# The first stage of a transformer layer: outputs squared and gated bank by bank, chunk states by one scan, a new order

## The chip, the cores and the metric

The kernel runs on one core of one Trainium2 chip. The metric is the device time of one execution in microseconds (us), the median of several. The engines of a core run side by side, each through its own list of instructions, and wait for one another by semaphores: TensorE (PE; its weight loads PEld), VectorE (DVE), ScalarE (ACT), GpSimd (POOL) and SyncE (SP), which issues most transfers.

## The reference

A layer over 8 sequences of 1024 tokens of width 256, in fp32. The kernel's first stage computes the gated linear attention and the projections of the softmax attention behind it:

```python
q, k, v = heads(x @ Wq), heads(x @ Wk), heads(x @ Wv)      # x is layer-normalised; 4 heads, 32 wide (v: 64)
g = maximum(log_sigmoid(x @ Wgk1 @ Wgk2 + bgk2) / 16, -3)
# per head, over the 1024 tokens:
S = S * exp(g_t) + k_t (outer) v_t ;  o_t = q_t @ S
o = o * rsqrt(mean(o * o over a head) + EPS) * rms_w * silu(x @ Wg)
x = x + o @ Wout
# then: layer norm and RMS norm of x, and its products with wq, wk, wv
```

Later stages, which the change leaves alone, are the softmax attention, its output projection with the router, and the experts.

## The kernel before

The function is `gla_and_projections`. It works on 16 halves of a sequence (N = 16, 512 tokens each, T = 4 tiles of 128). Each engine's list is a loop `for n in bodies` with n from -2 to 16. In body n an engine works on several halves: the front part (normalised input, projections, gate, chunk states) of half n + 1, the back part (outputs, gating, output projection, `x1`, the q and k projections of the softmax attention) of half n, and the values and last roundings of half n - 1. The order in each list is written out by hand and is the order of execution; a waiting instruction holds back all that stand behind it on its engine.

A half is cut into NC = 16 chunks of C = 32 tokens. Within a chunk the outputs come from scores (`AT`), between chunks from states `S`. The names that matter:

- TensorE: `outputs` (lines 701 and 704, the products with the states `Sbd` and with `AT`, two tiles a bank), `projection` z, q, k, `values_and_gate` (line 619), `gated_transposes` of `o_s` and `attention_transposes` of `xr` (line 625), `output_projection` (724), `key_transposes` (661), `scores` (674), `increments` (686: each chunk's addition to the state, in 4 banks, 4 chunks a bank), `attention_projection` (619, `a_wT`), `values` (619, `a_wT,a_xrT`), `input_transposes` (625, `a_xn`).
- VectorE: `squares` (360), `outputs` (374 and 377: times the root, times the gate), `gates` and `running_sums` (392 is a scan), `layer_sum` (`x1` and its statistics, 406 to 413), `decayed` (`kt`, `qt`, 422 and 423), `attention_input` (`xr`, 430), `within_chunks` (440: scores into `AT` under a mask, by bank), `attention_input_low` (447), `states` (474), `rests` (482).
- ScalarE: the copies out of PSUM, the gate's Abs, Exp and Ln (219 to 223), the exponentials of the decays (251 to 255), `states` (278: four copies of 8 chunks each, one a head, into the block-diagonal `Sbd`, and again four), `rounded` (287).
- GpSimd: powers of -1/2 for the roots (548 to 567), `kh` and `qh`.

`states` on VectorE is a chain of 16 instructions, in which each reads the state before it and the increment in PSUM:

```python
V_.scalar_tensor_tensor(S[:, c + 1], S[:, c], decay[:, c:c + 1], p_f[:, c % 4, (c // 4) * DV:(c // 4 + 1) * DV],
                        ALU.mult, ALU.add).then_inc(s["S_step"], 1)
```

ScalarE starts on the first four copies of `Sbd` once 7 steps are done. TensorE's `outputs` of tiles 0 and 1 wait for these four, those of tiles 2 and 3 for the other four.

## Time and profile before

| | us |
|---|---|
| median of three runs (lowest, highest) | 3053.11 (3050.43, 3057.81) |
| span of the profiled execution | 3058.2 |
| first stage, in the span | 0 to about 735 |
| busy in the span: PE, DVE, ACT, POOL | 2879.5, 2283.9, 1938.1, 688.5 |

The profile is one execution, taken by the hardware profiler; beside its span there is nothing that it times. The span is read by stages. The softmax attention (735 to 2050) is the longest, the experts (2325 to 3058) the next. In the first stage the page's row of busy tenths shows PE at 9 and DVE and ACT at 5 to 7, and the granted TensorE clock mostly at 9 tenths. So the clock is not full there all the time.

### The profile page before, as it was taken

The page shows a single profiled execution, that of the slowest core. Times are in us where ns is not written, and L with a number is a line of the kernel's source. Part 1 is how long each engine was busy: PE and PEld are TensorE (multiplying, and loading weights), DVE is VectorE, ACT ScalarE, POOL GpSimd, SP SyncE. Part 2 cuts the span into 40 slices and gives each one's busy share as a digit, 9 for nine tenths or more (in the row PEclk, how much of TensorE's full clock was granted, in tenths as well). Part 3 has the DMA queues.
Part 4 walks back from the last instruction along what each step waited for, and adds up shares of the span by engine and source line. Part 5 has one row for each costly group of instructions (what it writes and reads, how often), then busy time and mean ns, then how long its engine had stood idle before and what let it go on. Part 6 is the DMA issues. An engine that isn't in the chain of part 4 may idle for free. (4 is left out here: it accounts for less than half of the span.)

```text
span 3058.2 us, 63018 instructions
## 1 busy us (share of the span) xinstructions
PE 2879.5 (94%) x22889; PEld 1806.1 (59%) x22890; DVE 2283.9 (75%) x4031; ACT 1938.1 (63%) x3559; POOL 688.5 (23%) x965
## 2 busy tenths in 40 slices
PE   5999999986999999999999999999888999999998
PEld 4777777774333333333333333337777888888886
DVE  5777777764999999999999999967785454545443
ACT  3666666661888888888888888875543333333332
POOL 2222222222000000000000000001103555555554
PEclk7899999986999999999999999998889999999999
DMA  1223323223222222222222222217642333333332
GB/s 45 87 98 107 111 101 105 100 84 117 68 74 65 83 72 72 67 67 65 73 72 69 66 64 72 73 39 212 213 146 51 50 50 50 49 51 49 50 50 42
DMA packets 170745, 243.05 MB, mean 79 GB/s; under 512 B 30920, under 2 KB 118240, under 8 KB 170512
## 3 DMA queue, kind: packets, MB, share of 16 engines
q1 hardware_dynamic: 121920, 170.57, 18.4%
q0 software_dynamic: 31152, 52.33, 8.9%
q10 hardware_dynamic: 17440, 16.98, 1.7%
q8 instruction: 155, 2.54, 0.4%
q14 instruction: 78, 0.64, 0.1%
HBM read 126.53 MB, written 111.21 MB: 78 GB/s over the span
## 5 line engine op out<-in xcount | busy, mean ns | idle before, releaser
L1030 DVE TENSOR_REDUCE b_mxq<-b_p_m 128x1 f32<-128x1024 f32 x1024 | 1220.6, 1222 | 76.2 <-PE b_p_m L1057 67.2
L964 ACT ACTIVATE b_probs<-b_p_e 128x512 f32<-128x512 f32 x2048 | 1105.4, 597 | 140.7 <-PE b_p_e L1110 40.1
L1057 PE MATMUL b_p_m<-b_kst,b_qst 64*128 64x512 f32 x1536 | 568.2, 449 | 0.8 <-DVE b_mxq L1030 0.8
L1110 PE MATMUL b_p_e<-b_qst,b_kst 64*128 64x512 f32 x1536 | 559.6, 444 | 0.2 <-ACT b_probs L964 0.2
L1082 PE MATMUL b_p_o<-b_probs,b_vst 128*32 128x256 f32 x6160 | 481.9, 390 | 0.5 <-ACT b_probs L964 0.4
L1110 PEld LDWEIGHTS b_p_e<-b_qst,b_kst 64*128 64x128 f32 x1536 | 236.4, 184 | 312.3 <-ACT b_probs L964 266.0
L1849 ACT ACTIVATE d_act<-d_p_up 128x512 f32<-128x512 f32 x136 | 81.2, 597 | 490.7 <-PE d_p_up L1922 490.7
L1082 PEld LDWEIGHTS b_p_o<-b_probs,b_vst 128*32 128x32 f32 x6160 | 126.3, 108 | 243.4 <-issue 133.4
L1818 POOL DMA_INDIRECT out_dram<-d_y,d_to x136 | 217.7, 1601 | 216.8 <-DVE d_y L1883 204.1
L1937 PE MATMUL d_p_y<-w2T,d_hT 128*128 x1096 | 259.1, 379 | 0.8 <-ACT d_hT L1843 0.8
L1865 DVE TENSOR_SCALAR d_xh<-d_p_x,d_ln 128x128 fp32r<-128x128 f32 x272 | 82.9, 346 | 233.5 <-PE d_p_x L1916 233.5
L1922 PE MATMUL d_p_up<-up_hi,d_xh 128*128 x544 | 248.7, 457 | 3.5 <-DVE d_xl L1869 1.5
L1057 PEld LDWEIGHTS b_p_m<-b_kst,b_qst 64*128 64x128 f32 x1536 | 234.3, 185 | 15.7 <-DVE b_mxq L1030 12.4
L1937 PEld LDWEIGHTS d_p_y<-w2T,d_hT 128*128 128x128 f32 x1096 | 207.9, 190 | 34.7 <-issue 1.0
L1922 PE MATMUL d_p_up<-up_hi,d_xl 128*128 x544 | 216.2, 397 | 0.0
L1922 PE MATMUL d_p_up<-up_lo,d_xh 128*128 x544 | 215.3, 396 | 0.0
L1057 PE MATMUL b_p_m<-kst,qst 64*128 64x512 f32 x512 | 194.3, 463 | 10.1 <-DVEq L1021 7.6
L1110 PE MATMUL b_p_e<-qst,kst 64*128 64x512 f32 x512 | 187.0, 444 | 0.2
L1008 POOL DMA_DIRECT2D o_d<-b_oT x63 | 35.7, 567 | 658.1 <-ACT b_oT L954 658.1
L1883 DVE TENSOR_SCALAR d_y<-d_p_y,d_share 128x256 f32<-128x256 f32 x137 | 66.3, 484 | 127.7 <-PE d_p_y L1937 118.4
L1082 PE MATMUL b_p_o<-b_probs,vst 128*32 128x256 f32 x2048 | 160.3, 390 | 0.0
L1806 POOL DMA_INDIRECT d_xs<-xg_d,d_tok x133 | 134.0, 1007 | 109.2 <-POOL d_tok L1803 103.3
(319 smaller groups left out, 4628.5 us busy)
## 6 DMA issues: line engine op xcount, KB each, us to landing
b_qst<-qk_d SPq DMA_DIRECT2D x288, 64.0 KB
b_kst<-qk_d SPq DMA_DIRECT2D x288, 64.0 KB
qk_d<-a_hi SPq DMA_DIRECT2D x32, 512.0 KB, 2.8
qk_d<-a_lo SPq DMA_DIRECT2D x32, 512.0 KB, 3.8
v_d<-a_v_s SPq DMA_DIRECT2D x16, 1024.0 KB, 4.5
o_d<-b_oT POOLq DMA_DIRECT2D x63, 256.0 KB, 2.7
b_vst<-v_d SPq DMA_DIRECT2D x48, 256.0 KB
raw<-in_L_ffn_w_dram SPq DMA_DIRECT2D x24, 512.0 KB, 4.9
```

Of the source, the lines that this page charges most:

```text
L964: nc.scalar.activation(probs[(2 * step + e % 4 // 2) % BUFS][:, (e % 2) * 512:(e % 2 + 1) * 512], p_e[(slot(e) if more1 else e) % EB][:], ...
L1030: V_.reduce_max(mxq[half][:, h, qt:qt + 1], p_m[j % 2][:], AX.X).then_inc(s["m_red"], 1)
L1057: mm(p_m[j % 2][:, kh * 512:(kh + 1) * 512], qst[r][rows(h), qt * P:(qt + 1) * P], kst[r][rows(h), kh * 512:(kh + 1) * 512], start=True, s ...
L1082: last = mm(p_o[32 * (2 * h + a):32 * (2 * h + a) + 32, at:at + 256], vst[step // KT % RING][:, step % KT, h, :], probs[(2 * step + h) % B ...
L1110: mm(p_e[u % EB][:], kst[r][rows(h), kt * P:(kt + 1) * P], qst[r][rows(h), a * 512:(a + 1) * 512], start=True, stop=True).then_inc(s["e_ps ...
L1806: g.indirect_dma_start(xs[r][:], None, xg_d, bass.IndirectOffsetOnAxis(ap=tok[r][:, 0:1], axis=0)).then_inc(s[f"x_in{r}"], 16)
L1818: g.indirect_dma_start(out_d, bass.IndirectOffsetOnAxis(ap=to[r][:, 0:1], axis=0), y[r][:], None, compute_op=ALU.add).then_inc(s[f"y_out{r ...
L1849: nc.scalar.activation(act_s[r][:], p_up[r][:, 0], ACT.Silu).then_inc(s["act_done"], 1)
L1865: last = V_.tensor_scalar(xh[r][:, k], p_x[:, k], ln2[:, k:k + 1], None, ALU.mult)
L1883: V_.tensor_scalar(y[1 - r][:], p_y[:, 0:D], share[(q + 3) % 4][:, 0:1], None, ALU.mult).then_inc(s["y_done"], 1)
L1922: last = mm(p_up[r][:, u], x[r][:, k], w[:, bass.ds(e, 1), u, k, :].rearrange("p o n -> p (o n)"), start=(j == 0), stop=(j == 5))
L1937: last = mm(p_y[:, 0:D], hT[r][:, k], w2T[:, bass.ds(e, 1), k, :].rearrange("p o n -> p (o n)"), start=(k == 0), stop=(k == 3))
```

## The change

1. `outputs` raises a semaphore for each bank of two tiles. ScalarE squares bank by bank (`output_squares(n, 0)`, `(n, 1)`), VectorE sums bank by bank, and multiplies the outputs by the gate straight out of PSUM (`gated_outputs`); ScalarE's copy to `o_s` is gone. Roots are taken in halves, and the product with them comes last.
2. The states come from one scan of VectorE. `S`, `steps` and `added` have the shape [P, DV, NC + 1], the chunk innermost. ScalarE writes the decays to `steps` (repeated over the 64 values) and the increments to `added` (four copies, one a bank). The first column of each row of `steps` is 0 and that of `added` the carried state, so one scan over 64 x 17 = 1088 elements gives all states. ScalarE's eight copies to `Sbd` read `S` with the chunk outside and the value inside, which is a step of 17 floats, and all wait for the scan.
3. ScalarE loads the table set that holds both exp and ln ahead of the gate; Silu needs the other. That makes 2 table loads a body in place of 4.
4. TensorE's `values(n - 1, 1)` moves from between the q and k projections to behind the key transposes, and z goes ahead of `values(n - 1, 0)`. `attention_transposes` goes tile by tile, each tile after its own `xr`. GpSimd's `input_roots` finishes the root that `xr` needs before it begins the other.
5. The orders on ScalarE, VectorE and SyncE follow. `rounded(n, 2)` moves to the next body, behind the first squares; `layer_norm` moves to the next body.
6. The mask is built in `o2`, whose space is free at the start.

The core of the diff:

```diff
-    S = sb("S", [P, NC + 1, DV])
+    S, steps, added = (sb(n, [P, DV, NC + 1]) for n in ("S", "steps", "added"))
...
             store_projection(n - 1, 1, "st_k")
-            store_values(n - 1)
             if n == N - 1:
                 load_first_pair()
             store_sum(n)
+            store_values(n - 1)
...
-        def output_squares(h):
-            if not 0 <= h < N:
-                return
-            act.wait_ge(s["o_ps"], h + 1)
-            A.activation(o2[:].rearrange("p t d -> p (t d)"), p_g[:, 0:2].rearrange("p a c -> p (a c)"), ACT.Square, scale=DV ** -0.5).then_inc(s["o2_done"], 1)
-
-        def outputs(h):
-            if not 0 <= h < N:
-                return
-            A.copy(o_s[:].rearrange("p t d -> p (t d)"), p_g[:, 0:2].rearrange("p a c -> p (a c)")).then_inc(s["o_s_done"], 1)
-
-        def gate(f):
+        def output_squares(h, part):
+            if not 0 <= h < N:
+                return
+            act.wait_ge(s["o_ps"], 2 * h + part + 1)
+            A.activation(o2[:, 2 * part:2 * part + 2].rearrange("p t d -> p (t d)"), p_g[:, part], ACT.Square, scale=DV ** -0.5).then_inc(s["o2_done"], 1)
+
+        def gate_table(f):
+            if not 0 <= f < N:
+                return
+            A.preload_act_table_set("natural_log_exp_and_others")
...
+            act.wait_ge(s["cum_done"], f + 1)
+            A.activation(e_cum[:], cum[:], ACT.Exp)
+            A.activation(decay[:], cum[:].rearrange("p (c j) -> p c j", j=C)[:, :, C - 1], ACT.Exp).then_inc(s["exps"], 1)
             act.wait_ge(s["tail_done"], f + 1)
             A.activation(e_tail[:], tail[:], ACT.Exp).then_inc(s["exps_tail"], 1)
-            A.activation(e_out[:], rel[:], ACT.Exp, scale=-1.0)
-            A.activation(e_in[:], rel[:], ACT.Exp).then_inc(s["exps_rel"], 1)
-            A.activation(e_cum[:], cum[:], ACT.Exp)
-            A.activation(decay[:], cum[:].rearrange("p (c j) -> p c j", j=C)[:, :, C - 1], ACT.Exp).then_inc(s["exps"], 1)
+            act.wait_ge(s["rel_done"], f + 1)
+            A.activation(e_in[:], rel[:], ACT.Exp)
+            A.activation(e_out[:], rel[:], ACT.Exp, scale=-1.0).then_inc(s["exps_rel"], 1)
+
+        def decay_steps(f):
+            if not 0 <= f < N:
+                return
+            act.wait_ge(s["exps"], f + 1)
+            A.copy(steps[:, :, 1:], decay[:].rearrange("p (o c) -> p o c", o=1).to_broadcast([P, DV, NC])).then_inc(s["steps_done"], 1)
+
+        def increments(f):
+            if not 0 <= f < N:
+                return
+            if f > 0:
+                act.wait_ge(s["S_done"], f)
+            for c in range(4):
+                act.wait_ge(s["inc_ps"], 4 * f + c + 1)
+                last = A.copy(added[:, :, 1:].rearrange("p v (t b) -> p b t v", b=4)[:, c], p_f[:, c, 0:T * DV].rearrange("p (t v) -> p t v", t=T))
+            last.then_inc(s["added_done"], 1)
...
-            act.wait_ge(s["S_step"], f * NC + 8 * part + 7)
+            act.wait_ge(s["S_done"], f + 1)
             for h in range(H):
-                last = A.copy(Sbd[h * DK:(h + 1) * DK, 8 * part:8 * part + 8, h * DV:(h + 1) * DV], S[h * DK:(h + 1) * DK, 8 * part:8 * part + 8, :])
+                last = A.copy(Sbd[h * DK:(h + 1) * DK, 8 * part:8 * part + 8, h * DV:(h + 1) * DV], S[h * DK:(h + 1) * DK, :, 8 * part:8 * part + 8].rearrange("p v c -> p c v"))
...
         for n in bodies:
+            input(n + 1)
+            output_squares(n, 0)
+            rounded(n - 1, 2)
             rounded(n - 1, 3)
-            input(n + 1)
-            output_squares(n)
+            gate_table(n + 1)
+            output_squares(n, 1)
+            gate_absolute(n + 1)
             values(n - 1, 0)
-            outputs(n)
-            gate(n + 1)
-            values(n - 1, 1)
-            q_k(n + 1)
+            gate_exponential(n + 1)
+            query(n + 1)
+            gate_logarithm(n + 1)
+            key(n + 1)
             gated(n)
             decays(n + 1)
             values_and_gate(n + 1, range(T))
             keys(n + 1)
+            values(n - 1, 1)
+            decay_steps(n + 1)
             attention_input(n)
+            increments(n + 1)
             rounded(n, 0)
             rounded(n, 1)
             states(n + 1, 0)
-            rounded(n, 2)
             states(n + 1, 1)
...
-        def squares(h):
-            if not 0 <= h < N:
-                return
-            dve.wait_ge(s["o2_done"], h + 1)
-            V_.reduce_sum(ss[:], o2[:].rearrange("p t (h v) -> p (t h) v", h=H), AX.X).then_inc(s["ss_done"], 1)
+        def squares(h, part):
+            if not 0 <= h < N:
+                return
+            dve.wait_ge(s["o2_done"], 2 * h + part + 1)
+            V_.reduce_sum(ss[:, 8 * part:8 * part + 8], o2[:, 2 * part:2 * part + 2].rearrange("p t (h v) -> p (t h) v", h=H), AX.X).then_inc(s["ss_done"], 1)
+
+        def gated_outputs(h, part):
+            if not 0 <= h < N:
+                return
+            dve.wait_ge(s["o_ps"], 2 * h + part + 1)
+            dve.wait_ge(s["vg_taken"], h * T + T)
+            V_.tensor_tensor(o_s[:, 2 * part:2 * part + 2].rearrange("p t d -> p (t d)"), p_g[:, part],
+                             G[h % 2][:, 2 * part:2 * part + 2].rearrange("p t d -> p (t d)"), ALU.mult).then_inc(s["oG_done"], 1)
...
-        def outputs(h):
-            if not 0 <= h < N:
-                return
-            dve.wait_ge(s["rs_done"], h + 1)
-            dve.wait_ge(s["o_s_done"], h + 1)
-            ov = o_s[:].rearrange("p t (h v) -> p (t h) v", h=H)
-            V_.tensor_tensor(ov, ov, rs[:].rearrange("p (a o) -> p a o", o=1).to_broadcast([P, T * H, DV]), ALU.mult).then_inc(s["on_done"], 1)
-            dve.wait_ge(s["on_done"], h + 1)
-            dve.wait_ge(s["vg_taken"], h * T + T)
-            V_.tensor_tensor(o_s[:], o_s[:], G[h % 2][:], ALU.mult).then_inc(s["og_done"], 1)
+        def outputs(h, part):
+            if not 0 <= h < N:
+                return
+            dve.wait_ge(s["rs_done"], 2 * h + part + 1)
+            dve.wait_ge(s["oG_done"], 2 * h + part + 1)
+            ov = o_s[:, 2 * part:2 * part + 2].rearrange("p t (h v) -> p (t h) v", h=H)
+            V_.tensor_tensor(ov, ov, rs[:, 8 * part:8 * part + 8].rearrange("p (a o) -> p a o", o=1).to_broadcast([P, 2 * H, DV]), ALU.mult).then_inc(s["og_done"], 1)
...
-                last = V_.tensor_scalar(xr[:, t], x1[:, t], mvb[:, t, 0:1], roots[:, 1, t:t + 1], ALU.subtract, ALU.mult)
-            last.then_inc(s["xr_done"], 1)
+                V_.tensor_scalar(xr[:, t], x1[:, t], mvb[:, t, 0:1], roots[:, 1, t:t + 1], ALU.subtract, ALU.mult).then_inc(s["xr_done"], 1)
...
+        def carried(f):
+            if not 0 <= f < N:
+                return
+            if f > 0:
+                dve.wait_ge(s["S_done"], f)
+            if f % 2:
+                V_.tensor_copy(added[:, :, 0], S[:, :, NC]).then_inc(s["S_carry"], 1)
+            else:
+                V_.memset(added[:, :, 0], 0.0).then_inc(s["S_carry"], 1)
+
         def states(f):
-            if not 0 <= f < N:
-                return
-            dve.wait_ge(s["inc_ps"], f + 1)
-            dve.wait_ge(s["exps"], f + 1)
+
+            if not 0 <= f < N:
+                return
+            dve.wait_ge(s["S_carry"], f + 1)
+            dve.wait_ge(s["steps_done"], f + 1)
+            dve.wait_ge(s["added_done"], f + 1)
             if f > 0:
                 dve.wait_ge(s["Sbd_done"], 2 * f)
-            if f % 2:
-                dve.wait_ge(s["S_step"], f * NC)
-                V_.tensor_copy(S[:, 0], S[:, NC]).then_inc(s["S_carry"], 1)
-            else:
-                V_.memset(S[:, 0], 0.0).then_inc(s["S_carry"], 1)
-            for c in range(NC):
-                if c > 0:
-                    dve.wait_ge(s["S_step"], f * NC + c)
-                else:
-                    dve.wait_ge(s["S_carry"], f + 1)
-                V_.scalar_tensor_tensor(S[:, c + 1], S[:, c], decay[:, c:c + 1], p_f[:, c % 4, (c // 4) * DV:(c // 4 + 1) * DV],
-                                        ALU.mult, ALU.add).then_inc(s["S_step"], 1)
+            flat = [tile[:].rearrange("p v c -> p (v c)") for tile in (S, steps, added)]
+            V_.tensor_tensor_scan(flat[0], flat[1], flat[2], 0.0, ALU.mult, ALU.add).then_inc(s["S_done"], 1)
...
+            input_low(n + 1)
+            squares(n, 0)
+            gated_outputs(n, 0)
             rests(n - 1, (2, 3))
             if n + 2 > 0:
                 statistics(n + 2)
-            input_low(n + 1)
-            squares(n)
+            squares(n, 1)
+            gated_outputs(n, 1)
+            layer_norm(n - 1)
             gate_minimum(n + 1)
-            outputs(n)
+            outputs(n, 0)
+            outputs(n, 1)
             gates(n + 1)
             running_sums(n + 1)
             if n + 2 > 0:
...
             layer_sum(n)
             decayed(n + 1)
             attention_input(n)
+            carried(n + 1)
             within_chunks(n + 1)
             attention_input_low(n)
-            layer_norm(n)
             states(n + 1)
             rests(n, (0, 1))
...
-            g.tensor_scalar(roots[:, 1], mvb[:, :, 1], 1.0 + EPS, EPS * EPS, ALU.mult, ALU.add)
+            g.tensor_scalar(roots[:, 1], mvb[:, :, 1], 1.0 + EPS, EPS * EPS, ALU.mult, ALU.add).then_inc(s["roots_eps"], 1)
+            pool.wait_ge(s["roots_eps"], 2 * h + 1)
+            g.tensor_tensor(roots[:, 1], roots[:, 1], mhalf[:, 0:T], ALU.pow).then_inc(s["roots_done"], 1)
             g.tensor_scalar(roots[:, 0], mvb[:, :, 1], EPS, None, ALU.add).then_inc(s["roots_eps"], 1)
-            pool.wait_ge(s["roots_eps"], h + 1)
-            g.tensor_tensor(roots[:, 1], roots[:, 1], mhalf[:, 0:T], ALU.pow).then_inc(s["roots_done"], 1)
+            pool.wait_ge(s["roots_eps"], 2 * h + 2)
             g.tensor_tensor(roots[:, 0], roots[:, 0], mhalf[:, 0:T], ALU.pow).then_inc(s["root0_done"], 1)
...
-                pe.wait_ge(s["S_step"], f * NC)
+                pe.wait_ge(s["added_done"], f)
...
-            last.then_inc(s["inc_ps"], 1)
+                last.then_inc(s["inc_ps"], 1)
...
-            pe.wait_ge(s["og_done"], h + 1)
+            pe.wait_ge(s["og_done"], 2 * h + 2)
             if h > 0:
-                pe.wait_ge(s["v_done"], 2 * h)
+                pe.wait_ge(s["v_done"], 2 * h - 1)
+                pe.wait_ge(s["lo_done"], 4 * h)
...
-            pe.wait_ge(s["xr_done"], h + 1)
-            transposes(p_g[:, 2:4], xr, s["xrT_ps"], each=True)
+            if h > 0:
+                pe.wait_ge(s["v_done"], 2 * h)
+            for t in range(T):
+                pe.wait_ge(s["xr_done"], h * T + (t + 1))
+                for k in range(2):
+                    last = tr(p_g[:, 2 + k, t * P:(t + 1) * P], xr[:, t, k * P:(k + 1) * P], ident[:])
+            last.then_inc(s["xrT_ps"], 1)
...
         for n in bodies:
             outputs(n, (0, 1))
             outputs(n, (2, 3))
+            projection(n + 1, "z", 2, "z_ps")
             values(n - 1, 0)
-            projection(n + 1, "z", 2, "z_ps")
             projection(n + 1, "q", 0, "q_ps")
-            values(n - 1, 1)
             projection(n + 1, "k", 1, "k_ps")
             values_and_gate(n + 1, 0)
             gated_transposes(n)
...
             values_and_gate(n + 1, 2)
             values_and_gate(n + 1, 3)
             key_transposes(n + 1)
+            values(n - 1, 1)
             scores(n + 1)
             attention_transposes(n)
             increments(n + 1)
```

**TensorE, from the vg projections to the increments.** `a_wT,a_xrT` in a product 256 wide is `values`. Before:

```order
L724 MATMUL a_p_g<-a_Wout_s,a_ogT 128x256 x8
L619 MATMUL a_p_f<-a_W_f,a_xT 128x512 x4
L619 MATMUL a_p_f<-a_W_f,a_xTl 128x512 x2
L619 MATMUL a_p_f<-a_W_f,a_xT 128x512 x4
L619 MATMUL a_p_f<-a_W_f,a_xTl 128x512 x2
L661 MATMUL a_p_f<-a_ident,a_kh 128x128 x4
L674 MATMUL a_p_f<-a_qt,a_kt 128x128 x16
L625 MATMUL a_p_g<-a_ident,a_xr 128x128 x8
L686 MATMUL a_p_f<-a_V,a_khat 32x64 x64
```

The same place of the changed kernel, whose lines have other numbers:

```order
L670 MATMUL a_p_f<-a_W_f,a_xTl 128x512 x2
L711 MATMUL a_p_f<-a_ident,a_kh 128x128 x4
L670 MATMUL a_p_g<-a_wT,a_xrT 128x256 x4
L670 MATMUL a_p_g<-a_wT,a_xrTl 128x256 x2
L670 MATMUL a_p_g<-a_wT,a_xrT 128x256 x4
L670 MATMUL a_p_g<-a_wT,a_xrTl 128x256 x2
L724 MATMUL a_p_f<-a_qt,a_kt 128x128 x16
L785 MATMUL a_p_g<-a_ident,a_xr 128x128 x8
L736 MATMUL a_p_f<-a_V,a_khat 32x64 x64
```

Twelve matmuls of the earlier half's values now stand between the key transposes and the scores.

**ScalarE, from the copy of `khat` to the next body's first copies.** `a_hi` is `rounded`, `a_xT` the next half's input, `a_o` the squares. Before:

```order
L261 COPY a_khat<-a_p_f 128x512
L268 ACTIVATE a_xrT<-a_p_g,a_ln1w_s 128x512 x2
L287 CAST a_hi<-a_p_g 128x512 x2
L278 COPY a_Sbd<-a_S 32x8x64 x4
L287 CAST a_hi<-a_p_g 128x512
L278 COPY a_Sbd<-a_S 32x8x64 x4
L287 CAST a_hi<-a_p_g 128x512
L202 CAST a_xT<-a_p_f 128x1024
L208 ACTIVATE a_o<-a_p_g 128x1024
```

Now:

```order
L291 COPY a_khat<-a_p_f 128x512
L326 COPY a_v_s<-a_p_g 128x8x2x16 x2
L275 COPY a_steps<-a_decay 128x64x16
L298 ACTIVATE a_xrT<-a_p_g,a_ln1w_s 128x512 x2
L284 COPY a_added<-a_p_f 128x4x64 x4
L317 CAST a_hi<-a_p_g 128x512 x2
L308 COPY a_Sbd<-a_S 32x8x64 x8
L202 CAST a_xT<-a_p_f 128x1024
L208 ACTIVATE a_o<-a_p_g 128x512
L317 CAST a_hi<-a_p_g 128x512 x2
```

The copies to `steps` and `added` are new, the eight `Sbd` copies stand together, and two roundings have gone behind the next half's first copies.

**VectorE, from `kt` and `qt` to the rests.** Before:

```order
L422 TENSOR_TENSOR a_kt<-a_k_s,a_e_out 128x512
L423 TENSOR_TENSOR a_qt<-a_q_s,a_e_in 128x512
L430 TENSOR_SCALAR a_xr<-a_x,a_mvb,a_roots 128x256 x4
L440 COPY_PREDICATED a_AT<-a_maski,a_p_f 128x512 x4
L447 SCALAR_TENSOR_TENSOR a_xrTl<-a_p_g,a_ln1w_s,a_xrT 128x512 x2
L454 COPY norm<-a_roots 128x4
L455 SCALAR_TENSOR_TENSOR norm<-a_mvb,a_roots 128x4
L468 MEMSET a_S 128x64
L474 SCALAR_TENSOR_TENSOR a_S<-a_S,a_decay,a_p_f 128x64 x16
L482 TENSOR_TENSOR a_lo<-a_p_g,a_hi 128x512 x4
```

Now:

```order
L464 TENSOR_TENSOR a_kt<-a_k_s,a_e_out 128x512
L465 TENSOR_TENSOR a_qt<-a_q_s,a_e_in 128x512
L472 TENSOR_SCALAR a_xr<-a_x,a_mvb,a_roots 128x256 x4
L504 COPY a_added<-a_S 128x64
L481 COPY_PREDICATED a_AT<-a_maski,a_p_f 128x512 x4
L488 SCALAR_TENSOR_TENSOR a_xrTl<-a_p_g,a_ln1w_s,a_xrT 128x512 x2
L518 SCALAR_TENSOR_TENSOR a_S<-a_steps,a_added 128x1088
L525 TENSOR_TENSOR a_lo<-a_p_g,a_hi 128x512 x2
```

One scan (shown here as SCALAR_TENSOR_TENSOR, as the other scan is) stands where the 16 steps stood.

## Rows read from the trace of the kernel before

**Rows 1.** Timeline of TensorE, one body: start us, length us, instructions, [wait before]

```profile
393.76 0.64 PE L701 MATMUL a_p_g<-a_Sbd,a_qh 128*32 128x256 f32 x8
...
404.36 0.64 PE L619 MATMUL a_p_g<-a_wT,a_xrT 128*128 128x256 f32 x4
...
405.80 1.10 PE L619 MATMUL a_p_f<-a_xT,a_W_f 128*128 128x512 f32 x4
...
414.40 1.28 PE L619 MATMUL a_p_f<-a_W_f,a_xT 128*128 128x512 f32 x4
...
417.40 0.60 PE L661 MATMUL a_p_f<-a_ident,a_kh 128*128 128x128 f32 x4
419.15 1.17 PE L674 MATMUL a_p_f<-a_qt,a_kt 32*128 32x128 f32 x32 [1.15 <-DVE a_qt L423]
422.68 1.47 PE L625 MATMUL a_p_g<-a_ident,a_xr 128*128 128x128 f32 x8 [2.35 <-DVE a_xr L430]
...
426.71 2.07 PE L619 MATMUL a_p_g<-a_xrT,a_wT 128*128 128x512 f32 x4
...
432.49 1.07 PE L619 MATMUL a_p_g<-a_xrT,a_wT 128*128 128x512 f32 x4
...
433.85 1.04 PE L625 MATMUL a_p_f<-a_ident,a_xn 128*128 128x128 f32 x8
434.81 0.64 PE L701 MATMUL a_p_g<-a_Sbd,a_qh 128*32 128x256 f32 x8
```

**Rows 2.** Stretches: length, busy of PE, PEld, DVE, ACT, POOL; granted clock; DMA

```profile
420.30:422.70 2.40, 0.05 (x4) 0.03 (x1) 2.40 (x5) 0.00 (x0) 2.17 (x2) 1.00 0.15 50
...
426.70:429.40 2.70, 2.70 (x10) 2.15 (x7) 2.27 (x9) 0.00 (x0) 0.00 (x0) 0.50 0.02 6
```

**Rows 3.** Timeline of VectorE in the same body

```profile
418.37 0.68 DVE L423 TENSOR_TENSOR a_qt<-a_q_s,a_e_in 128x512 f32<-128x512 f32 x1
420.29 2.33 DVE L430 TENSOR_SCALAR a_xr<-a_x,a_mvb,a_roots 128x256 f32<-128x256 f32 x4 [1.24 <-POOL a_roots L566]
422.54 2.57 DVE L440 COPY_PREDICATED a_AT<-a_maski,a_p_f 128x512 f32<-128x512 int32 x4
425.02 1.38 DVE L447 SCALAR_TENSOR_TENSOR a_xrTl<-a_p_g,a_ln1w_s,a_xrT 128x512 fp32r<-128x512 f32 x2
```

**Rows 4.** Timeline of GpSimd in the same body

```profile
418.56 0.58 POOL L564 TENSOR_SCALAR a_roots<-a_mvb 128x4 f32<-128x4 f32 x1
419.22 1.04 POOL L566 TENSOR_TENSOR a_roots<-a_roots,a_mhalf 128x4 f32<-128x4 f32 x1
```

**Rows 5.** Timeline of ScalarE in the same body

```profile
431.85 2.49 ACT L278 COPY a_Sbd<-a_S 32x512 f32<-32x512 f32 x4
```

**Rows 6.** Groups by line and shape: count | busy us, mean ns of one | wait

```profile
L550 POOL TENSOR_TENSOR a_rs<-a_rs,a_mhalf 128x16 f32<-128x16 f32 x16 | 46.9, 2930 | 1.3
L392 DVE TENSOR_TENSOR_SCAN a_cum<-a_keep,a_zm 128x512 f32<-128x512 f32 x16 | 19.6, 1225 | 0.5
L360 DVE TENSOR_REDUCE a_ss<-a_o 128x16 f32<-128x1024 f32 x16 | 19.6, 1222 | 25.7 <-ACT a_o L208 25.7
L254 ACT ACTIVATE a_e_cum<-a_cum 128x512 f32<-128x512 f32 x16 | 9.8, 615 | 0.0
L255 ACT ACTIVATE a_decay<-a_cum 128x16 f32<-128x16 f32 x16 | 3.4, 214 | 0.0
...
L1396 DVE TENSOR_REDUCE slots<-c_where 128x8 f32<-128x64 f32 x16 | 4.3, 268 | 0.5
...
L1288 ACT ACTIVATE c_ed<-c_diff 128x4 f32<-128x4 f32 x16 | 3.1, 193 | 7.5 <-DVE c_diff L1368 7.5
```

**Rows 7.** Stretches, as in rows 2: `outputs` in body 0 and in body 1

```profile
58.90:70.40 11.50, 11.50 (x65) 7.88 (x65) 1.22 (x1) 1.29 (x2) 0.00 (x0) 0.50 0.00 0
106.30:112.60 6.30, 6.30 (x66) 4.45 (x65) 3.75 (x11) 4.00 (x7) 0.00 (x0) 1.00 0.48 179
```

**Rows 8.** Timeline of TensorE in body 15, where the gated transposes begin

```profile
700.39 0.90 PE L625 MATMUL a_p_g<-a_ident,a_o_s 128*128 128x128 f32 x3 [5.34 <-DVE a_o_s L377]
```

51 lines of the change are left out of this document (30 added, 21 removed).

## Prediction

> **What bounds the kernel now.** I read the page first, then TensorE's timeline of one body, then the clock by stretch, then the engines it waits for. The change touches only the first stage, whose body runs 15 times from n = 0 to n = 14 with all its parts. Its start, the first matmul of `outputs`, stands at 393.76 and again at 434.81, so a body takes 41.05 us [rows 1]. The profile's span is 3058.2 us, 5.1 us (0.17%) over the median of the runs; I work out a saving on the span and take it from the median.
>
> In a body TensorE is nearly always busy. It waits twice: 1.15 us ahead of the scores (for `qt`) and 2.35 us ahead of the transposes of `xr` [rows 1]. Inside the second wait the granted clock is still 1.00; from 426.70 to 429.40, in the first attention projection, it is 0.50 [rows 2]. The fourth projection takes 1.36 us (432.49 to 433.85), which is full clock; all four take 7.14 (426.71 to 433.85) instead of 5.44 [rows 1]. So a body loses 3.5 us to waits and at least 1.7 us to the clock. Nothing else holds TensorE; a gain has to come out of these 5.2 us.
>
> **What the change does there.** All times from here are counted from E, the end of the output projection (414.40 in the trace).
>
> Before: `qt` is ready at E + 4.65 and the scores run from there; `roots` at E + 5.86; the four `xr` at E + 5.89 to 8.22; transposes from E + 8.28; increments to E + 12.31; then projections, input transposes, and the next `outputs` at E + 20.41 [rows 1, 3, 4].
>
> *The moved product.* `values(n-1, 1)` took 1.44 us (404.36 to 405.80) ahead of E [rows 1]. It now fills the wait ahead of the scores: vg and key transposes end at about E + 3.6, the product at E + 5.05, just after `qt` (E + 4.65). The stretch ahead of E shortens by 1.44, and the first wait is gone. The scores end at E + 6.2.
>
> *Roots and `xr`.* GpSimd now does one preparatory step less ahead of the first pow: 0.66 us (418.56 to 419.22) [rows 4]. `xr` starts at E + 5.25 and each quarter takes 0.58, since GpSimd is busy beside it as before; the last ends at E + 7.58. Transposes go tile by tile, so only two are left then: they end at E + 7.85, with waits of 0.7 in all.
>
> *Chunks and increments.* The four predicated copies (2.57 us, [rows 3]) follow at E + 7.8, after a small carry copy, and end at E + 10.35. A bank of increments waits for each. Increments never ran at full clock in a body; between 0.3 and 0.65 a bank, I take 0.65, since 2.6 us for four is what the half-clock row shows and the copies set the pace anyway. They end at E + 11.05 against 12.31.
>
> *If TensorE alone decided,* four projections at full clock and the input transposes (5.44 + 0.96) put the next `outputs` at E + 17.5 (before 20.41), and with the 1.44 the body would be 36.7 us: 4.4 less.
>
> *The state chain, which decides next.* The 16 steps were interleaved with the Sbd copies. Now the increments are copied to `added` (last bank E + 11.5), the scan waits for that and for `xrTl` (E + 10.35 + 1.38), and then all eight Sbd copies wait for the whole scan. The scan over 1088 elements costs 1225 x 1088/512, less fixed cost, about 2.45 [rows 6]: done at E + 14.2. ScalarE first rounds the second projection (E + 14.5). Then come the eight copies.
>
> *What one copy costs now.* A copy takes 0.62 us reading `S` in order (2.49 for four, [rows 5]). Now it reads with a step of 17 floats. Two rows show such reads. ScalarE's `decay` reads 16 elements 32 floats apart in 214 ns; 4 elements in order take 193 and 512 take 615, which puts 16 in order at 203: 0.7 ns more per element. VectorE's reduction over 64 elements 8 floats apart takes 268 ns; from 0.68 us at 512 and 1222 at 1024, 64 in order would take about 214: 0.84 ns more per element [rows 3, 6]. For 512 elements that is 0.36 to 0.43 us on top, so a copy costs 0.98 to 1.05; the other bound is no surcharge, 0.62. Both rows point the same way, so I take 1.04.
>
> The Trainium skill (SBUF — State Buffer, the note on cachelines in the section on the DMA port swizzle) says that each access that crosses to a new 16-byte line pays a penalty. The two rows agree for reads. By that page the writes to `added` would pay as well, some 0.2 us on the chain a body, which no row shows.
>
> With 1.04, four copies end at E + 18.7 and eight at E + 22.9. `outputs` of tiles 0 and 1 can start at 18.7, those of tiles 2 and 3 wait until 22.9, and end 3.1 later at E + 26.0 (before: 20.41 + 6.30 = 26.7). From there to the next E it is 14.33 - 1.44 = 12.9. The body: 38.9 us, 2.15 less. So TensorE's two old waits shrink and a new one of about 2.2 us stands ahead of and inside `outputs`.
>
> *The rest lies beside other work.* Squaring and gating by bank saves one ScalarE pass over the outputs and adds fixed costs on VectorE; with the pow in halves (2930 ns for 16 columns, 1.04 for 4: about 1.7 for 8) the gated outputs are ready about when the gated transposes come, within 0.3 us either way. Two of four table loads go from ScalarE, beside TensorE's projections: nothing. The `steps` copy (1024 elements, about 1.0) fits into ScalarE's wait for the `xrT` transposes. The queue of stores moves one store behind another, with its ring free for most of a body: nothing. VectorE loses 5 us of steps and gains 2.45.
>
> *Ends of the stage.* In body 15 nothing hides the chain from outputs to gated transposes, 8.3 us before (to 700.39 [rows 8]); square and reduction of half the data, half the pow and one multiplication make it about 4.3. Earlier roots and `xr` by tile save about 1 more. The start gains nothing, since eight slow copies take the place of the interleaved ones. Together 5.
>
> **Sum.** 15 x 2.15 + 5 = 37: 3058.2 - 37 = 3021.2 on the span, **3016** against the median.
>
> **The rivals.**
> *Copies cost no more than before, or little* (22%). Then TensorE decides: 15 x 4.4 + 5 + 1.5 at the start = 72, 2981 if the clock holds throughout; where it still falls in every second body at a cost of about 2.5, 53, so 3000. Against it speak the two strided rows; for it, that one is only 16 elements long.
>
> *The clock falls in the increments as it does now* (28%). What precedes its fall now are waits of 1.15 and 2.35 us with the scores between [rows 1, 2]. The new stretch has waits of 0.7 and 0.4 and thin work (transposes one pair at a time, increments at the pace of VectorE), so it is not clear that it holds. If it falls, two to four projections run at half clock, the second ends up to 2.7 later, and the Sbd copies behind its rounding shift by 1.3 to 2.7: a body of 40.2 to 41.6. Over 15 bodies with the 5 of the end: 3036 to 3056; I name 3044.
>
> *Slower: the clock falls in the new wait ahead of `outputs`* (14%). `outputs` at half clock take 11.5 us (58.90 to 70.40) against 6.3 at full, and in that whole stretch the clock stayed at 0.50 [rows 7]. With a wait of 1.2, half of `outputs`, and another of 1.0, work is thinner than now. Falling there costs 2.6 for tiles 2 and 3, and 2 to 3 in the projections behind, 4 to 5 against a gain of 2.15. It decides once over 40% of the bodies fall: in all of them 3053 + 15 x 2.4 - 5 = 3084; in half of them about 3050.
>
> *The change doesn't do what it says* (1%): the order on ScalarE shows two loads a body, so this is closed but for the clock.
>
> **How the numbers follow.** Forecast 35%: 3016, with its own range 3006 to 3028 (a copy at 0.98 to 1.08 and a few bodies with a clock loss). Copies fast 22%: 2981 to 3000. Clock as before 28%: 3036 to 3056. Slower 14%. The range 2986 to 3056 leaves out about 2 in 10. A measurement tells 0.2% (6 us) from no change, so faster means under 3047: all of the first two cases and two thirds of the third, 76%; within 0.2%: 11%; slower: 13%.
>
> **What would show it.** Sbd copies at 1.0 us in the group view (0.62 would make it the first rival); TensorE waiting for them ahead of the `Sbd` matmuls; no wait ahead of the scores; the body's period at 38.9; the scan at 2.4; the granted clock at 1.00 through the projections. A clock of 0.50 from the increments on means the second rival, 0.50 in `outputs` the third. I am wrong in kind if TensorE waits for something else, the gated outputs above all.

## The result, and the profile after

| | before | after |
|---|---|---|
| median, us | 3054.08 | 3072.43 |
| ratio to before, 95% interval | | 1.0056 (1.0039 to 1.0073) |
| span of the profiled execution | 3058.2 | 3068.5 |
| busy PE, DVE, ACT | 2879.5, 2283.9, 1938.1 | 2909.2, 2238.9, 1997.0 |

The change made the kernel 17 us (0.6%) slower, where 37 us less were forecast. (Two slow executions, 3717 us of the changed kernel and 11511 us of fill_second below, are left out of the ratios; without them the medians are 3071.4 and 3031.2.) VectorE lost 45 us of work, as it should. TensorE, whose matmuls are as many as before, is busy 30 us longer, and the two products of `outputs` account for all of it: the one with `Sbd` grew from 42.7 to 52.8 us, the one with `AT` from 74.2 to 94.5. The granted clock below shows why.

```profile
L704 PE MATMUL a_p_g<-a_V,a_AT 128*128 128x64 f32 x512 | 74.2, 290 | 0.0
L754 PE MATMUL a_p_g<-a_V,a_AT 128*128 128x64 f32 x512 | 94.5, 344 | 0.0
```

First the groups of after that answer to [rows 6] and [rows 3, 5]: count | busy us, mean ns of one | wait.

```profile
L308 ACT COPY a_Sbd<-a_S 32x512 f32<-32x512 f32 x128 | 140.3, 1096 | 4.2 <-DVE a_S L518 2.6
L751 PE MATMUL a_p_g<-a_Sbd,a_qh 128*32 128x256 f32 x512 | 52.8, 492 | 38.8 <-issue 33.7 <-ACT a_Sbd L308 5.1
L518 DVE TENSOR_TENSOR_SCAN a_S<-a_steps,a_added 128x1088 f32<-128x1088 f32 x16 | 38.8, 2424 | 8.6 <-ACT a_added L284 8.6
L284 ACT COPY a_added<-a_p_f 128x256 f32<-128x256 f32 x64 | 36.9, 617 | 4.5 <-PE a_p_f L736 4.4
L472 DVE TENSOR_SCALAR a_xr<-a_x,a_mvb,a_roots 128x256 f32<-128x256 f32 x64 | 22.2, 406 | 14.9 <-POOL a_roots L614 14.9
```

A strided `Sbd` copy takes 1096 ns, the scan 2424, and TensorE now waits 38.8 us ahead of the products with `Sbd`. Most of that is booked as "issue", which names no releaser; the experiments below show that it is the copies.

TensorE's timeline in one body, as in [rows 1]. E is the end of the output projection, 502.81:

```profile
482.57 0.64 PE L751 MATMUL a_p_g<-a_Sbd,a_qh 128*32 128x256 f32 x8 [1.52 <-issue]
...
487.00 0.64 PE L751 MATMUL a_p_g<-a_Sbd,a_qh 128*32 128x256 f32 x8 [1.15 <-issue]
...
502.81 1.28 PE L670 MATMUL a_p_f<-a_W_f,a_xT 128*128 128x512 f32 x4
...
507.75 1.17 PE L724 MATMUL a_p_f<-a_qt,a_kt 32*128 32x128 f32 x32
508.93 1.31 PE L785 MATMUL a_p_g<-a_ident,a_xr 128*128 128x128 f32 x8
510.57 2.49 PE L736 MATMUL a_p_f<-a_V,a_khat 32*32 32x64 f32 x128 [0.34 <-DVE a_AT L481]
512.99 1.22 PE L670 MATMUL a_p_g<-a_xrT,a_wT 128*128 128x512 f32 x4
514.03 1.04 PE L670 MATMUL a_p_g<-a_xrTl,a_wT 128*128 128x512 f32 x2
514.87 1.91 PE L670 MATMUL a_p_g<-a_xrT,a_wT 128*128 128x512 f32 x4
...
522.74 0.64 PE L751 MATMUL a_p_g<-a_Sbd,a_qh 128*32 128x256 f32 x8 [1.50 <-issue]
523.30 1.11 PE L754 MATMUL a_p_g<-a_V,a_AT 128*128 128x64 f32 x8
524.35 1.08 PE L751 MATMUL a_p_g<-a_Sbd,a_qh 128*32 128x256 f32 x8
525.36 1.97 PE L754 MATMUL a_p_g<-a_V,a_AT 128*128 128x64 f32 x8
```

The two old waits, ahead of the scores and of the transposes of `xr`, are gone. Two new ones stand ahead of `outputs` (1.5 us) and between its halves (1.15 us). The second projection runs at half clock (1.91 for four, 1.08 at full clock). The `outputs` at 482.57 ran at full clock throughout; those at 522.74 slowed down from 524.35 on. ScalarE's rows of the same body, behind its copies to `added`:

```profile
515.16 0.59 ACT L317 CAST a_hi<-a_p_g 128x512 fp32r<-128x512 f32 x1 [1.40 <-PE a_p_g L670]
517.69 0.58 ACT L317 CAST a_hi<-a_p_g 128x512 fp32r<-128x512 f32 x1 [1.95 <-PE a_p_g L670]
518.17 8.88 ACT L308 COPY a_Sbd<-a_S 32x512 f32<-32x512 f32 x8
```

It waits 1.95 us for the second projection and then copies for 8.9 us.

The clock over `outputs` in each body shows which of the two happened. Six of the fifteen stretches that begin where `outputs` begin in bodies 1 to 15, columns as in [rows 2]; the granted clock is the third number from the right:

```profile
100.53:107.53 7.00, 5.85 (x60) 3.96 (x60) 1.60 (x2) 6.92 (x9) 0.00 (x0) 1.00 0.03 9
140.63:147.63 7.00, 7.00 (x46) 4.73 (x47) 1.61 (x2) 6.92 (x9) 0.00 (x0) 0.60 0.01 3
185.67:192.67 7.00, 5.85 (x60) 3.96 (x60) 1.60 (x2) 6.92 (x9) 0.00 (x0) 1.00 0.00 1
226.46:233.46 7.00, 5.85 (x48) 4.04 (x48) 1.60 (x2) 6.92 (x9) 0.00 (x0) 0.80 0.00 0
...
652.54:659.54 7.00, 7.00 (x47) 4.73 (x47) 1.61 (x2) 6.92 (x9) 0.00 (x0) 0.60 0.01 3
698.19:705.19 7.00, 7.00 (x41) 4.39 (x42) 0.53 (x1) 5.46 (x7) 0.00 (x0) 0.51 0.00 0
```

Of bodies 1 to 14, seven show 1.00 and take 40.1 to 40.8 us; seven show 0.60, 0.61, 0.80 or 0.81 and take 44.7 to 45.7. Together they take 597.7 us (100.53 to 698.19), where the same fourteen took 579.4 before. The rest of the +10.3 between the two profiled spans: `outputs` of body 0 start 1.8 earlier (57.16; before [rows 7]), body 0 is 4.0 shorter (43.4 against 47.35), the stage's end is 0.2 longer, and what follows the stage is 2.4 shorter: 18.3 - 1.8 - 4.0 + 0.2 - 2.4 = 10.3.

### The profile page after: what moved, and what is told of

It reads as the page before. It is cut to its first block and busy times, and to the rows that moved or that the text cites. A ratio compares the mean times of both kernels' runs of the same rounds, so it can differ in the third digit from the quotient of the medians.

```text
span 3068.5 us, 62992 instructions
## 1 busy us (share of the span) xinstructions
PE 2909.2 (95%) x22889; PEld 1819.1 (59%) x22890; DVE 2238.9 (73%) x3840; ACT 1997.0 (65%) x3608; POOL 689.9 (22%) x997
## 5 line engine op out<-in xcount | busy, mean ns | idle before, releaser
L1114 PE MATMUL b_p_m<-kst,qst 64*128 64x512 f32 x512 | 194.3, 463 | 10.2 <-DVEq L1078 7.7
```

The costliest lines, as they stand in the source:

```text
L1114: mm(p_m[j % 2][:, kh * 512:(kh + 1) * 512], qst[r][rows(h), qt * P:(qt + 1) * P], kst[r][rows(h), kh * 512:(kh + 1) * 512], start=True, s ...
```

## Experiments

All times are medians; ratios are to the kernel before, whose median was 3056.7 to 3057.6 beside these runs.

| kernel | from | us | ratio, 95% interval |
|---|---|---|---|
| flat_reads | after | 2988.36 | 0.9784 (0.9768 to 0.9801) |
| steps16 | after | 2982.90 | 0.9770 (0.9751 to 0.9789) |
| scan_only | before | 3124.41 | 1.0226 (1.0209 to 1.0244) |
| fill | after | 3059.08 | 1.0013 (1.0000 to 1.0026) |
| copies_twice | steps16 | 3084.70 | 1.0093 (1.0075 to 1.0111) |
| early_copies | after | 3047.04 | 0.9970 (0.9956 to 0.9983) |
| split_copies | after | 2985.81 | 0.9763 (0.9747 to 0.9779) |
| values_back | steps16 | 3022.54 | 0.9885 (0.9867 to 0.9903) |
| fill_both | after | 3030.60 | 0.9914 (0.9898 to 0.9931) |
| squares_whole | steps16 | 3007.61 | 0.9842 (0.9826 to 0.9859) |
| roots_back | steps16 | 3040.99 | 0.9951 (0.9935 to 0.9968) |
| tables_back | steps16 | 3014.41 | 0.9862 (0.9845 to 0.9878) |
| fill_second | after | 3033.68 | 0.9925 (0.9902 to 0.9948) |
| powers_back | steps16 | 3023.27 | 0.9892 (0.9874 to 0.9910) |

**The copies.** flat_reads takes the stride away and nothing else:

```diff
-                last = A.copy(Sbd[...], S[h * DK:(h + 1) * DK, :, 8 * part:8 * part + 8].rearrange("p v c -> p c v"))
+                last = A.copy(Sbd[...], S[h * DK:(h + 1) * DK].rearrange("p v c -> p (v c)")[:, 512 * part:512 * part + 512].rearrange("p (c v) -> p c v", c=8))
```

> The changed kernel, but the eight copies to Sbd read S as it lies in memory (512 numbers in a row) instead of with a step of 17 floats; so the states that reach outputs are the wrong ones, and a step of the computation is left out, while every instruction, its size and its waits stay. Theory (the strided copies): in the changed kernel a copy takes 1.10 us, eight of them 8.9, and outputs wait 1.5 us for the first four and 1.15 for the others. Read in order a copy should take 0.62 as before, the eight 5.0; both waits go, and with them the fall of the clock inside outputs. Body 38.6 to 39.6 us, time 3010 to 3035. Rival (the thin stretch of per-tile transposes and increments is what makes the clock fall, in outputs too): copies at 0.62, but about half of the bodies still at 44 to 45; 3050 to 3065.

Measured 2988.4. The groups, and `outputs` in a middle body:

```profile
L308 ACT COPY a_Sbd<-a_S 32x512 f32<-32x512 f32 x128 | 78.9, 616 | 4.2 <-DVE a_S L518 2.6
L751 PE MATMUL a_p_g<-a_Sbd,a_qh 128*32 128x256 f32 x512 | 42.7, 406 | 3.6 <-ACT a_Sbd L308 3.2 <-issue 0.4
```

```profile
470.12 0.64 PE L751 MATMUL a_p_g<-a_Sbd,a_qh 128*32 128x256 f32 x8
471.72 0.64 PE L751 MATMUL a_p_g<-a_Sbd,a_qh 128*32 128x256 f32 x8
473.33 0.64 PE L751 MATMUL a_p_g<-a_Sbd,a_qh 128*32 128x256 f32 x8
```

The copies fall to 616 ns, both waits go, the granted clock is 1.00 over `outputs` in bodies 1 to 15, and most bodies take 37.3 us. It came out even better than the theory's 3010. The stride in the `Sbd` copies is worth 84 us, though all 128 are only 61 us shorter in sum.

**The states undone.** steps16 is the changed kernel with the states as before: `S` with the value innermost, no `steps`, `added` and their copies, 16 instructions:

```diff
-            decay_steps(n + 1)
...
-            increments(n + 1)
...
-            act.wait_ge(s["S_done"], f + 1)
+            act.wait_ge(s["S_step"], f * NC + 8 * part + 7)
...
-            V_.tensor_tensor_scan(flat[0], flat[1], flat[2], 0.0, ALU.mult, ALU.add).then_inc(s["S_done"], 1)
+            for c in range(NC):
...
+                V_.scalar_tensor_tensor(S[:, c + 1], S[:, c], decay[:, c:c + 1], p_f[:, c % 4, (c // 4) * DV:(c // 4 + 1) * DV],
+                                        ALU.mult, ALU.add).then_inc(s["S_step"], 1)
```

> The changed kernel with the states as they were before: 16 steps of VectorE from PSUM, no steps and added, S with the value innermost, the first four Sbd copies from the seventh step on. The new order, the squares and gating by bank and the table set stay. Theory (the strided copies and the wait for the whole scan make the loss): no wait ahead of outputs, the granted clock 1.00 in outputs in every body, a body of 38.6 to 39.8 us, so 3010 to 3035, faster than both kernels. Rival (the new order itself makes the loss): about half of the bodies at 44 to 45, time 3050 to 3075.

2982.9, faster than both kernels (2.3% under before). Nearly all of its bodies take 36.2 or 37.3 us; TensorE in one:

```profile
466.71 1.03 PE L655 MATMUL a_p_f<-a_ident,a_xn 128*128 128x128 f32 x8
467.68 0.64 PE L730 MATMUL a_p_g<-a_Sbd,a_qh 128*32 128x256 f32 x8
```

`outputs` follow the input transposes without a wait. So everything in the change but the scan form is worth some 74 us, and the scan form with its strided copies takes back 90. The scan as such costs next to nothing: flat_reads has it too, without the stride, and is within 6 us of steps16.

**The scan form alone** on the kernel before, with the diff's parts for `S`, `steps`, `added`, the scan, the `Sbd` copies and the mask:

```diff
+            decay_steps(n + 1)
             attention_input(n)
+            increments(n + 1)
             rounded(n, 0)
             rounded(n, 1)
             states(n + 1, 0)
             rounded(n, 2)
             states(n + 1, 1)
```

> The kernel before with only the states changed: steps and added, one scan, eight strided Sbd copies (four, a rounding, four), mask in o2. Theory (the strided copies behind the scan make the loss): nothing of the order gives time back, so outputs start and end about 3 us later a body, 15 x 3.1 = 47 and some for the clock: 3090 to 3135. Rival (the scan form costs nothing by itself, the order does): 3050 to 3060.

3124.4. Waits of 1.5 and 1.8 us appear ahead of and inside `outputs`, beside the two old ones:

```profile
425.69 0.64 PE L723 MATMUL a_p_g<-a_Sbd,a_qh 128*32 128x256 f32 x8 [1.52 <-issue]
...
430.72 0.64 PE L723 MATMUL a_p_g<-a_Sbd,a_qh 128*32 128x256 f32 x8 [1.76 <-issue]
```

**Length or stride?** copies_twice puts a block of about the same length on ScalarE (16 copies, 9.2 us in a body) without scan and stride:

```diff
             for h in range(H):
+                A.copy(twice[h * DK:(h + 1) * DK, part], S[h * DK:(h + 1) * DK, 8 * part:8 * part + 8, :].rearrange("p c v -> p (c v)"))
                 last = A.copy(Sbd[...], S[...])
```

> steps16, but with each of the eight Sbd copies a second copy of the same size and speed into a tile that nobody reads. There is no scan and no strided access in it; ScalarE alone is busy for 16 x 0.62 = 9.9 us where the changed kernel's eight strided copies take 8.9. Theory (the length of ScalarE's copies behind the second rounding sets outputs): TensorE waits ahead of and inside outputs again, the clock falls in outputs in many bodies, and the time is that of the changed kernel or somewhat above: 3070 to 3110. Rival (the scan as such, its wait for all increments, or strided accesses that disturb other engines make the loss): waits short, 2985 to 3010.

3084.7: the changed kernel's time and pattern came back, with bodies of 40.3 to 47.4 us and falls inside `outputs`. So it is how long ScalarE is busy behind the second rounding, however it is made so.

**The copies on two engines.** split_copies keeps scan and stride and gives VectorE the copies of heads 2 and 3:

```diff
             states(n + 1)
+            states_half(n + 1, 0)
             rests(n, (0, 1))
+            states_half(n + 1, 1)
```

> The changed kernel, scan and strided layout kept, but VectorE makes the copies of heads 2 and 3 (two ahead of its rests 0 and 1, two behind), ScalarE those of heads 0 and 1. Theory (only the length of the copies on one engine holds outputs): 4 x 1.1 = 4.4 us in place of 8.9, no wait ahead of outputs, the body of 37.3 us that the kernel with reads in order has: 2985 to 3005. Rival (VectorE is late with its rests, for which outputs wait as well, or its own strided copies are much slower than 1.1 us): 3020 to 3060.

2985.8, not to be told from steps16. Its groups show something that nobody had expected: the same strided read on the two engines.

```profile
L308 ACT COPY a_Sbd<-a_S 32x512 f32<-32x512 f32 x64 | 70.6, 1103 | 3.4 <-DVE a_S L518 2.6
L527 DVE COPY a_Sbd<-a_S 32x512 f32<-32x512 f32 x64 | 39.7, 621 | 1.6
```

No run has VectorE's copy in order, so what the stride costs VectorE isn't shown. Its one-input operation over 512 numbers in order (L428 in the changed kernel) takes 0.43 us, so it may pay some 0.2, an estimate.

**What delays the copies' start.** early_copies moves one line, since ScalarE's second rounding waits for a projection that runs at half clock:

```diff
-            rounded(n, 1)
             states(n + 1, 0)
+            rounded(n, 1)
             states(n + 1, 1)
```

> The changed kernel with the first four Sbd copies ahead of ScalarE's rounding of the second projection. Counted from E, the end of the output projection, the scan is done at E + 13.5 and the copies now start at E + 15.4, since they stand behind that rounding, and the projection it waits for runs at half clock. Theory (the half-clock projection delays the copies through this rounding): first four done at E + 17.9, outputs of tiles 0 and 1 from E + 19.2 (behind the rounding and VectorE's rest of it), all copies at E + 23, outputs end at E + 26.1 and not 27.4: 1.2 us a body off, and some falls of the clock fewer: 3035 to 3060. Rival (rounding and rest then come late and hold outputs as long): 3065 to 3080.

3047.0: a body without a fall mostly takes 39.0 to 39.5 us instead of 40.1, and the clock falls in `outputs` of 4 of the bodies 1 to 14 instead of 7. `outputs` now wait for VectorE's rest, as expected, and hardly for the second four copies. The wait for the rest is at most 1.1 us in nine of these bodies, none of which falls, and 2.7 in the other five, of which four fall. One without:

```profile
390.99 0.64 PE L751 MATMUL a_p_g<-a_Sbd,a_qh 128*32 128x256 f32 x8 [1.14 <-DVE a_lo L525]
...
394.64 0.64 PE L751 MATMUL a_p_g<-a_Sbd,a_qh 128*32 128x256 f32 x8 [0.38 <-issue]
```

**The waits filled.** fill does the 8 transposes of the next input twice, ahead of `outputs`. fill_second puts 8 transposes of `V`, whose result is not used, between the halves of `outputs`. fill_both does both. The copies are as long as in the changed kernel. The fill of the second wait:

```diff
             outputs(n, (0, 1))
+            for t in range(T if 0 <= n < N else 0):
+                for k in range(2):
+                    tr(p_f[:, 3, t * P:(t + 1) * P], V[:, t, k * P:(k + 1) * P], ident[:])
             outputs(n, (2, 3))
```

> The changed kernel, with the 8 transposes of the next input done twice. They stand right ahead of outputs, so the second set (0.8 to 1.0 us) lies in the wait of 1.5 us and leaves 0.5 to 0.7 of it; the other wait, of 1.15 us inside outputs, stays. Theory 1 (the idle time ahead of outputs is what lets the clock fall in about half of the bodies): most of the seven or so bodies of 45 us go to 40: 3040 to 3055. Theory 2 (TensorE's idle time in this one place doesn't decide; it is the whole stretch, or the second wait): 3068 to 3080, and as many bodies of 45 us as without.

> The changed kernel with both new waits of TensorE filled: the 8 transposes of the next input done twice ahead of outputs (as in the run with one wait filled), and 8 more transposes, of V into a bank that is free there, between outputs of tiles 0 and 1 and those of tiles 2 and 3, where 1.15 us are idle. The copies to Sbd end when they did. Theory (what TensorE does in these waits is what lets its clock fall inside outputs): nearly all bodies at 40.1 to 40.5 in place of half of them at 45: 3035 to 3050. Rival (the thin increments ahead decide, however the waits are filled): half of the bodies still at 45, 3060 to 3080.

> The changed kernel with only the wait between outputs of tiles 0 and 1 and those of tiles 2 and 3 filled, by 8 transposes of V into a free bank; the wait of 1.5 us ahead of outputs stays. With both filled no outputs ran at half clock (3031); with the first alone filled the median was 3059, with none 3072. Theory 1 (the two waits count together): some of the bodies still fall, 3045 to 3062. Theory 2 (the wait that stands inside outputs decides alone): 3028 to 3036. Theory 3 (the wait ahead decides alone): 3065 to 3080.

Measured: none filled 3072, the first 3059, both 3031, the second alone 3034. fill_second, `outputs` of one body:

```profile
378.31 0.64 PE L751 MATMUL a_p_g<-a_Sbd,a_qh 128*32 128x256 f32 x8 [1.53 <-issue]
...
381.42 1.04 PE L813 MATMUL a_p_f<-a_ident,a_V 128*128 128x128 f32 x8
382.74 0.64 PE L751 MATMUL a_p_g<-a_Sbd,a_qh 128*32 128x256 f32 x8 [0.27 <-issue]
```

Work that nobody needs, put into the second wait, makes the kernel 1.3% faster than the changed one: the granted clock is 1.00 over `outputs` in all of bodies 1 to 14, and most bodies take 38.5 or 40.1 us. The wait of 1.5 us ahead of `outputs` is still there and does no harm by itself. So theory 2 on record for fill_second holds (3028 to 3036), and the theory that the wait ahead of `outputs` is what matters, on record for fill, is wrong.

The first wait seems to have a say in where the clock falls. The profiled execution of fill was its longest (3084.9 us, with ten falls in bodies 1 to 14), so it doesn't stand for the median, but in none of the ten does the clock fall ahead of the second wait, as it did in five of seven in the changed kernel. One of them, where it falls right behind:

```profile
191.49 1.08 PE L754 MATMUL a_p_g<-a_Sbd,a_qh 128*32 128x256 f32 x8 [1.15 <-issue]
```

And the two waits are not enough for a fall. scan_only has longer ones, 1.5 and 1.8 us, and over the 8 us from the start of `outputs` its clock is 1.00 in ten of the bodies 1 to 14, 0.94 in three and 0.78 in one. Two of them:

```profile
381.22:389.22 8.00, 6.24 (x63) 4.35 (x64) 3.08 (x11) 6.38 (x7) 0.00 (x0) 1.00 0.11 41
425.69:433.69 8.00, 6.24 (x59) 4.23 (x60) 3.08 (x11) 6.37 (x7) 0.00 (x0) 0.94 0.11 41
```

So one thing stays open. In the changed kernel's two bodies with 0.80 or 0.81 both waits are there and the clock falls behind the second; in the five with 0.60 or 0.61 it is down before the second wait would come (524.35 above), and yet filling the second removes these falls too. The runs show that filling it removes the falls, not how, nor what a fall needs besides the waits.

**What the rest of the change is worth,** each part undone alone in steps16 (2982.9). values_back puts the values' second product back between the q and k projections:

```diff
             projection(n + 1, "q", 0, "q_ps")
+            values(n - 1, 1)
             projection(n + 1, "k", 1, "k_ps")
...
             key_transposes(n + 1)
-            values(n - 1, 1)
```

> steps16 with the values' second product back between the q and k projections, on TensorE and ScalarE. Theory (the product fills the wait ahead of the scores, as the prediction had it): the 1.44 us stand in the body's full stretch again and the wait for qt returns; 1.2 to 1.5 us a body, 15 x 1.35 = 20: 2998 to 3010, or up to 3030 if the clock falls in the scores as well. Rival (the stretch behind it is set by roots and xr anyway): 2980 to 2990.

3022.5: 40 us, where the theory had 20, or up to 47 if the clock fell in the scores as well, which it doesn't (1.17 us below is full clock). The wait for `qt` is back:

```profile
485.74 1.17 PE L703 MATMUL a_p_f<-a_qt,a_kt 32*128 32x128 f32 x32 [1.18 <-DVE a_qt L446]
```

Its bodies take 37.6 to 41.4 us. By the pages TensorE is busy 2854.7 us in steps16 and 2869.4 in values_back: of the 40 us by which the span grew (2979.0 to 3019.2), 15 are slower matmuls and 25 idle time. So the clock has a part in it.

roots_back puts back GpSimd's order and the transposes behind all four `xr`; powers_back only the first of the two:

```diff
-            g.tensor_scalar(roots[:, 1], mvb[:, :, 1], 1.0 + EPS, EPS * EPS, ALU.mult, ALU.add).then_inc(s["roots_eps"], 1)
-            pool.wait_ge(s["roots_eps"], 2 * h + 1)
-            g.tensor_tensor(roots[:, 1], roots[:, 1], mhalf[:, 0:T], ALU.pow).then_inc(s["roots_done"], 1)
+            g.tensor_scalar(roots[:, 1], mvb[:, :, 1], 1.0 + EPS, EPS * EPS, ALU.mult, ALU.add)
             g.tensor_scalar(roots[:, 0], mvb[:, :, 1], EPS, None, ALU.add).then_inc(s["roots_eps"], 1)
-            pool.wait_ge(s["roots_eps"], 2 * h + 2)
+            pool.wait_ge(s["roots_eps"], h + 1)
+            g.tensor_tensor(roots[:, 1], roots[:, 1], mhalf[:, 0:T], ALU.pow).then_inc(s["roots_done"], 1)
```

> steps16 with GpSimd's two preparatory steps ahead of the first power again, and the transposes of xr after all four quarters, as before. Theory 1 (as the prediction had it, 0.66 us earlier, and quarters hidden one behind the other): 0.66 and about 0.7 a body, 15 x 1.3: 3000 to 3005. Theory 2 (the order of the powers also sets whether GpSimd works beside xr, which took 2.33 us for the four before and takes 1.39 in the new kernels): transposes from E + 8.2 in place of E + 6.1, 2.1 a body: 3012 to 3030.

> steps16 with GpSimd's two preparatory steps ahead of the first power again, while the transposes of xr stay tile by tile. In the traces of before and of roots_back one quarter of xr in each body takes 1.35 us and the other three 0.41; the long one starts just behind the start of GpSimd's product qh (421.21 and 421.3 in before). In the changed kernel xr ends as qh starts, and no quarter takes over 0.43. Theory 1 (0.66 us later is enough to put the last quarter beside qh; the predicated copies and the increments behind it are late by 1.6, and TensorE's clock falls on that wait): the long quarter is back, and the time is near that of roots_back, 3020 to 3041. Theory 2 (transposes by tile hide most of it): 2990 to 3007. Theory 3 (the long quarter is not due to qh): quarters at 0.41, 2985 to 2995.

3041.0 and 3023.3: theory 2 of the one and theory 1 of the other as far as the long quarter goes, though roots_back cost more than 3030 (of the 61 us by which its profiled span grew, 31 are TensorE's busy time, so again the clock). The four quarters of `xr` in one body of powers_back and of all bodies of after (count: shortest/median/longest ns, first and last start):

```profile
L453 DVE TENSOR_SCALAR a_xr<-a_x,a_mvb,a_roots x4: 407/410/1357, 482.8 to 483.8; 128x256 f32<-128x256 f32 x4
```

```profile
L472 DVE TENSOR_SCALAR a_xr<-a_x,a_mvb,a_roots x64: 394/400/428, 87.8 to 728.5; 128x256 f32<-128x256 f32 x64
```

Three quarters take 0.41 us and the last 1.36. In roots_back it starts at 495.3, beside GpSimd's product `qh` (495.24, 1.27 us). In after `qh` starts at 509.73, when `xr` (508.35, 1.39 us in all) is at its end, and no quarter is long. The 0.66 us saved ahead of the first power thus bring 1.3: the power then takes 1.33 us instead of 1.04, so `xr` starts only 0.35 earlier, and the long quarter's 0.94 is saved. The transposes by tile are worth the 18 us between powers_back and roots_back.

squares_whole puts back the squares, sums, roots and gating of four tiles at once, with ScalarE's copy `o_s`:

```diff
-            output_squares(n, 0)
...
-            output_squares(n, 1)
+            output_squares(n)
             gate_absolute(n + 1)
             values(n - 1, 0)
+            outputs(n)
```

> steps16 with the squares, their sums, the roots and the gating of all four tiles at once, as before, and ScalarE's copy of the outputs back. Theory (the bank-wise form is needed because the moved product no longer stands between outputs and the gated transposes): that chain took 8.4 us uncovered in body 15 before, and in steps16 the work that covers it takes 7.1 (473.97 to 481.05), so TensorE waits 1.3 to 1.4 us a body, and 4 more at the end of the stage: 3003 to 3015, more if the clock falls on it. Rival (the gating by bank is hidden either way but for the end): 2985 to 2990.

3007.6, in the theory's range. TensorE waits ahead of the gated transposes in each body:

```profile
496.30 1.09 PE L649 MATMUL a_p_g<-a_ident,a_o_s 128*128 128x128 f32 x8 [1.21 <-DVE a_o_s L400]
```

tables_back drops the one load of the common set:

```diff
-            gate_table(n + 1)
```

> steps16 without the load of the table set that holds exp and ln together: ScalarE then loads a set for each of them, 4 loads a body in place of 2, 2 x 1.28 us more. Theory (these lie beside TensorE's projections, nobody waits): 2981 to 2988. Rival (the gate's chain to qt and kt is late with them, and the scores wait): 1 to 2.6 a body, 3000 to 3020.

3014.4, so the theory that nobody waits is wrong by 31 us, and the time lies in the rival's range. ScalarE's timeline: three of the four loads now stand between the gate and the decays.

```profile
469.09 1.28 ACT L225 ACT_TABLE_LOAD   x1
470.39 0.63 ACT L225 ACTIVATE a_e_in<-a_za 128x512 f32<-128x512 f32 x1
470.92 0.57 ACT L237 COPY a_q_s<-a_p_f 128x512 f32<-128x512 f32 x1
471.51 1.28 ACT L231 ACT_TABLE_LOAD   x1
...
475.04 1.28 ACT L263 ACT_TABLE_LOAD   x1
476.33 0.63 ACT L263 ACTIVATE a_e_cum<-a_cum 128x512 f32<-128x512 f32 x1
```

TensorE waits 0.29 us ahead of the output projection and 0.40 ahead of the scores in that body. Four other waits, up to 2.6 us long, stand inside the increments, and five of the bodies 1 to 14 take 40 us or more. Of the 40 us by which its profiled span grew (2979.0 to 3019.0), 19.5 are TensorE's busy time (2854.7 to 2874.2), which is its clock, and the other 20.5 idle time.

## The prediction, step by step

**Right: the values' product, roots, transposes, increments.** Counted from E, the scores start at 4.94 with no wait (forecast about 5.05), the transposes of `xr` end at 7.4 (7.85), the increments at 10.2 (11.05), the scan at 13.6 (14.2). They came earlier than forecast for one wrong term above all: "each quarter takes 0.58, since GpSimd is busy beside it as before" took a mean of three at 0.41 and one at 1.36 for the price of each. The long one belongs to `qh`, and the 0.66 us moved `xr` ahead of it. (Against it, the first power took 1.33 us instead of 1.04, so that `xr` started at 5.54 and not 5.25.) With reads in order the whole of this stands: 37.3 us a body in flat_reads (forecast 36.7), 2988 in the 2981 to 3000 of the rival in which the copies cost no more than before.

**Wrong by a little: the copy.** 1.04 was forecast, 1.10 measured: eight cost 8.9 us instead of 8.3. Both strided rows pointed the right way. ScalarE's `decay` row [rows 6] gave 0.7 ns more per number, and the copy pays 0.94. VectorE's reduction was misread: the line through 0.68 us at 512 and 1222 ns at 1024 gives 206 ns for 64 in order, not 214, which would be 1.12 for a copy. That this is near the 1.10 is luck, since the row is of another engine, and split_copies shows VectorE making the same strided copy in 621 ns.

The Trainium skill (SBUF — State Buffer, the note on cachelines in the section on the DMA port swizzle) lets every crossing to a new line cost. ScalarE's read agrees (1096 against 616 ns). So does its write to `added`, 617 ns for 256 numbers at stride, where its copies to `V`, 256 in order, take about 370 (1.0 us more a body, beside the increments but for the last). For VectorE's read no run shows the price in order, so whether it agrees is open.

**The step that failed: what the clock does, and when the copies begin.** "The second projection" was taken at full clock, so copies from E + 14.5. It ran at half clock, as in the second rival, its rounding ended at 518.27, and the copies began at E + 15.4. That and the 1.10 put `outputs` at E + 19.9 (forecast 18.7) and the end of the copies at E + 24.2 (22.9): a body of 40.1 in place of 38.9. early_copies took the first back and gave 39.0. This is the second rival at its mild end, and by itself it would still have been a gain: fourteen bodies at 40.3 instead of 597.7 us are 33 less, a span of 3035, 23 under before.

The rest is the third rival, and its mechanism was priced rightly: a fall in `outputs` costs 4.8 us (45.1 against 40.3; forecast 4 to 5), and 7 of 14 bodies fall. (Its "it decides once over 40% of the bodies fall" doesn't follow from its own figures: 2.15 gained against 4 to 5 lost puts the line at about half, where it names 3050, still under before.) Its time (3050 in half of the bodies) was worked out from a body of 38.9. The two rivals are no alternatives: the half-clock projection delays the copies, so the wait ahead of `outputs` is longer (1.5 us, where the third rival had 1.2). From 40.3 and half of the bodies at 45.1, 42.7 a body, the same sum gives 3073, where 3072 was measured (its 5 us for the ends came from the start, as told below). I gave them 28% and 14% apart, and no chance to both. The forecast should have asked, for a wait that it put itself ahead of `outputs` (2.2 us "ahead of and inside"), why the clock should hold there when it fell behind waits of 1.15 and 2.35 us in the same body before [rows 1, 2]. It could not have been certain of a fall either: in scan_only the clock mostly holds behind waits as long.

**Ends.** At the end of the stage the chain from `outputs` to the gated transposes shrank to 4.4 us (709.58 to 714.03; forecast 4.3), but `outputs` of body 15 ran at half clock, 11.4 us (698.19 to 709.58) instead of 6.3, so nothing was left. The start, put at nothing, gained 5.8.

**"The rest lies beside other work."** By tables_back this holds only for where TensorE waits, not for its time: 2 x 1.28 us of loads on an engine that TensorE rarely waits for were worth 31 us, half of it waits of TensorE in several small places and half its clock. And squares_whole shows that the gating by bank, put at nothing within a body, is needed there: the moved product no longer covers the chain (7.1 us of cover for 8.4).

## What to carry over

A step that is moved off one engine can land on another as a block that nothing overlaps: count how long the receiving engine is busy in a row, with the price of its own access pattern, and measure whether another engine reads that pattern faster. When a change opens a wait on TensorE, price the clock behind it together with the wait, and ask of two risks in one chain whether the one brings on the other. Before a large change is judged as a whole, run it with its most doubtful part undone: here that version, steps16, was the gain.

## What the runs showed of the hardware

- ScalarE reads 512 numbers of 4 bytes with a step of 17 in 1096 to 1103 ns and in order in 616. VectorE reads the same with that step in 621; its price in order is in no run.
- Four `xr` quarters of VectorE take 0.41 us each, but 1.36 when they begin just behind the start of GpSimd's product of two 512-wide tiles, which takes 1.27: the long quarter ends 0.15 us after the product (422.62 and 422.47 before). Beside GpSimd's powers of 4 numbers they were not slowed, nor were the predicated copies (0.72) beside that product.
- 8 transposes without use, 1.04 us, in a wait of TensorE made a kernel 39 us faster (3072 to 3034), since the clock then held in every `outputs` of bodies 1 to 14.
- Undone one by one from the fastest kernel, the product's place, the powers' order, the gating by bank and the table set cost 40, 40, 25 and 31 us. By the pages TensorE's busy time grew by 15, 24, -1 and 20 of the 40, 43, 26 and 40 us by which the profiled spans grew: with three of the four, a third to somewhat over half of the price was the clock, not waits.
- Two waits of TensorE, 1.5 and 1.8 us, inside 8 us left the granted clock at 1.00 in ten of fourteen bodies of scan_only, while waits of 1.5 and 1.15 us went with a fall in seven of fourteen of the changed kernel.
